# Cross-attention on one core: value products on stacked high and low parts, row sums on GpSimd, low probabilities on VectorE

## What is computed

```python
lat = layer_norm(latents, ln_lat_g, ln_lat_b)          # 4 x 128 x 512
ctx = layer_norm(context, ln_ctx_g, ln_ctx_b)          # 4 x 2048 x 512
q = (lat @ Wq).reshape(b, n, 16, 64).transpose(0, 2, 1, 3)
k, v = jnp.split(ctx @ Wkv, 2, axis=-1)                # 16 heads of 64 each
k = apply_rope(k, cos, sin)
attn = jnp.einsum('bhnd,bhsd->bhns', q, k) * 64 ** -0.5
attn = jax.nn.softmax(jnp.clip(attn, -11.0, 11.0), axis=-1)
out = jnp.einsum('bhns,bhsd->bhnd', attn, v)
```

## Time and profile before

| | us |
|---|---|
| median of three runs | 1448.81 |
| lowest, highest | 1445.45, 1450.21 |
| the profiled execution | 1454.4 |
| its span, first to last instruction | 1452.7 |
| the attention loop in it | about 83 to 1150 |

### The profile page before, as it was taken

How to read it: one execution, slowest core, us unless ns; L and a number is a source line. 1 busy time by engine, 2 the same in 40 slices (tenths; PEclk the granted TensorE clock), 3 DMA queues, 4 the chain that set the end, 5 groups by cost and what they waited for, 6 DMA issues and landing times. The chain is left out here.

```text
span 1452.7 us, 25242 instructions
## 1 busy us (share of the span) xinstructions
PE 1394.5 (96%) x8758; PEld 1139.3 (78%) x8758; DVE 850.0 (59%) x1420; ACT 797.3 (55%) x1237; POOL 833.6 (57%) x723
## 2 busy tenths in 40 slices
PE   5899999999999999999999999999998889999998
PEld 3578888888788888878888888888887566766664
DVE  6456565666466566655565666656554356657564
ACT  3356566665566665656666656656555312346652
POOL 3267677776667776766777777777765324110002
PEclk9999999999999999999999999999999989899999
DMA  7567766766666676656677666776767380369994
GB/s 241 178 118 130 123 118 110 132 116 135 114 120 123 111 130 110 139 100 129 113 131 122 123 130 118 130 123 107 138 107 163 116 326 0 131 219 365 357 370 150
DMA packets 115219, 218.44 MB, mean 150 GB/s; under 512 B 13312, under 2 KB 49152, under 8 KB 108928
## 3 DMA queue, kind: packets, MB, share of 16 engines
q1 hardware_dynamic: 111920, 209.00, 63.8%
q0 software_dynamic: 1280, 4.20, 0.9%
q10 hardware_dynamic: 1872, 3.41, 0.6%
HBM read 132.67 MB, written 16.78 MB: 103 GB/s over the span
## 5 line engine op out<-in xcount | busy, mean ns | idle before, releaser
L605 POOL TENSOR_TENSOR p_parts<-probs,p_parts 128x512 fp32r<-128x512 f32 x256 | 340.3, 1349 | 252.2 <-ACT p_parts L660 252.2
L660 ACT ACTIVATE p_parts<-probs 128x512 fp32r<-128x512 f32 x256 | 147.7, 625 | 245.5 <-PE banks L914 237.9
L768 DVE TENSOR_TENSOR probs<-banks,probs 128x1024 f32<-128x1024 f32 x128 | 156.7, 1224 | 164.1 <-ACT probs L668 164.1
L709 ACT ACTIVATE probs<-probs 128x1024 f32<-128x1024 f32 x128 | 135.9, 1062 | 142.6 <-POOL probs L612 142.5
L866 PE MATMUL banks<-wv_hi,x_hi 128*128 128x512 f32 x512 | 208.5, 407 | 4.9 <-PEq L170 4.9
L867 PE MATMUL banks<-wv_lo,x_hi 128*128 128x512 f32 x512 | 202.8, 396 | 0.0
L881 PE MATMUL banks<-x_hi,wk_hi 128*128 128x512 f32 x512 | 201.8, 394 | 0.0
L868 PE MATMUL banks<-wv_hi,x_lo 128*128 128x512 f32 x512 | 201.8, 394 | 0.0
L883 PE MATMUL banks<-x_hi,wk_lo 128*128 128x512 f32 x512 | 199.6, 390 | 0.0
L882 PE MATMUL banks<-x_lo,wk_hi 128*128 128x512 f32 x512 | 199.3, 389 | 0.0
L910 PE MATMUL banks<-p_parts,v_hi 128*65 128x128 f32 x1024 | 192.0, 224 | 0.6 <-POOL p_parts L605 0.6
(11 more groups left out here) (291 smaller groups left out, 2694.5 us busy)
## 6 DMA issues: line engine op xcount, KB each, us to landing
queries<-q_scratch SPq DMA_DIRECT2D x256, 128.0 KB, 6.0
keys<-wo_room SPq DMA_DIRECT2D x128, 256.0 KB, 5.6
keys<-turned_odd SPq DMA_DIRECT2D x128, 256.0 KB, 5.6
row_room<-in_ctx SPq DMA_DIRECT2D x64, 256.0 KB, 6.2
wo_room<-in_down SPq DMA_DIRECT2D x10, 1024.0 KB, 7.1
...
```

Source lines behind the costliest of these rows:

```text
L605: nc.gpsimd.tensor_tensor(p_parts[:, 1, j, :], probs[:, pair % 2, j, :], p_parts[:, 0, j, :].bitcast(F32), ALU.subtract).then_inc(p_lo_rea ...
L768: nc.vector.tensor_tensor(mine, ps_s[:, :, :, 0, :].rearrange("p j i n -> p (j i) n"), mine, ALU.add).then_inc(s_taken, 1)
```

## The change

Four things. **Values:** `v_parts` holds the high and the low part of a head's values side by side, 128 columns, with no column of ones; one product takes them both by the high and low parts of the probabilities, which now lie side by side in `p_parts` (256 columns). Its output has 128 partitions, 64 of high values and 64 of low values, by 256 columns. The quarter of low by low is computed and left unused. 8 products in place of 24. **Row sums:** GpSimd adds the probabilities of a pair over the four row tiles and the chunks into `totals` by three additions (`add_halves`, `add_totals`), and `turn_sums` turns those too. **Low probabilities:** one subtraction of 1024 elements on VectorE, between the normalisation and `take_scores`; the high part is one copy on ScalarE. **Sums:** `add_values` adds the left half of the bank into all 128 partitions of `acc` and then the right half (low probabilities) of the upper 64 (high values); `finish` adds the two halves of partitions after the turn. To make room, the queries have two slots instead of four, and each pair's load is issued in a step of its own.

```diff
-QUERY_SLOTS = 4
+QUERY_SLOTS = 2
...
-        v_lo = sb("v_lo", [P, ROW_TILES, HEADS, DHEAD], F32R)
         queries = sb("queries", [P, QUERY_SLOTS, 2, 2, QUERIES], F32R)
         probs = sb("probs", [P, 2, 2, CHUNK])
-        p_parts = sb("p_parts", [P, 2, 2, CHUNK], F32R)
-        acc = sb("acc", [DHEAD + 1, HEADS, QUERIES])
...
+        acc = sb("acc", [2 * DHEAD, HEADS, QUERIES])
+
+        totals = sb("totals", [P, HEADS, QUERIES])
+        halves = sb("halves", [P, 2, ROW_TILES // 2, QUERIES])
         recip = sb("recip", [P, 2])
+        total = sb("row_total", [P, 2])
...
-        sums = ps_o[0:DHEAD + 1, 0:2 * QUERIES].rearrange("p (j n) -> p j n", n=QUERIES)
+
+        sums = ps_o.rearrange("p (j w n) -> p j w n", j=2, n=QUERIES)
         rows["ps_tr"] = ps_o.rearrange("p (t n) -> p t n", n=P)
-        turned_sums = ps_s[:, 0, 0:2, 0, 0:DHEAD + 1]
+        turned_sums, turned_totals = ps_s[:, 0, 0:2, 0, :], ps_s[:, 0, 0:2, 1, :]
...
+                    wait(sp, k_ready, BATCH * BSTEPS - STEPS)
...
+                if exists(b, t - 2):
+
+                    if exists(b, t - SCORE_LAG):
+                        wait_alone(sp, s_ready, b * BSTEPS + (t - SCORE_LAG + 1))
+                    load_queries(b, t - 2)
+                if isinstance(b, int) and b == BATCH - 1:
+                    early_loads(t)
...
-                    if exists(b, t - 3):
-
-                        wait_alone(sp, s_ready, b * BSTEPS + (t - SCORE_LAG))
...
-                    for pair in (t - 3, t - 2):
-                        if exists(b, pair) and exists(b, t - 2):
-                            load_queries(b, pair)
-                    if exists(b, t - 2) and not exists(b, t):
-
-                        load_queries(b, t - 1)
...
-            def low_probs(b, pair):
+            def add_halves(b, pair):
+
                 if exists(b, pair):
-                    for j in range(2):
-                        wait(pool, p_hi_ready, b * (2 * BSTEPS) + (2 * pair + j + 1))
-                        nc.gpsimd.tensor_tensor(p_parts[:, 1, j, :], probs[:, pair % 2, j, :], p_parts[:, 0, j, :].bitcast(F32),
-                                                ALU.subtract).then_inc(p_lo_ready, 1)
+                    mine = probs[:, pair % 2].rearrange("p j (i n) -> p j i n", n=QUERIES)
+                    wait(pool, probs_ready, b * BSTEPS + (pair + 1))
+                    wait(pool, totals_ready, 2 * (b * BSTEPS + pair))
+                    nc.gpsimd.tensor_tensor(halves[:], mine[:, :, 0:2, :], mine[:, :, 2:4, :], ALU.add).then_inc(halves_ready, 1)
+
+            def add_totals(b, pair):
+                if exists(b, pair):
+                    n = b * BSTEPS + pair
+                    m = pair % STEPS
+                    mine = totals[:, 2 * m:2 * m + 2, :]
+                    wait(pool, halves_ready, n + 1)
+                    if pair // STEPS % CHUNKS == 0:
+                        for j in range(2):
+                            nc.gpsimd.tensor_tensor(mine[:, j, :], halves[:, j, 0, :], halves[:, j, 1, :], ALU.add).then_inc(totals_ready, 1)
+                    else:
+                        nc.gpsimd.tensor_tensor(halves[:, :, 0, :], halves[:, :, 0, :], halves[:, :, 1, :], ALU.add).then_inc(totals_ready, 1)
+                        wait(pool, totals_ready, 2 * n + 1)
+                        nc.gpsimd.tensor_tensor(mine, mine, halves[:, :, 0, :], ALU.add).then_inc(totals_ready, 1)
...
-                low_probs(b, t - VALUE_LAG)
+                add_halves(b, t - VALUE_LAG)
+                add_totals(b, t - VALUE_LAG)
                 clip(b, t - SCORE_LAG)
...
-                    for j in range(2):
-                        nc.scalar.activation(p_parts[:, 0, j, :], probs[:, pair % 2, j, :], ACT.Copy).then_inc(p_hi_ready, 1)
+                    nc.scalar.activation(p_parts[:, :, :, 0, :].rearrange("p j i n -> p (j i) n"),
+                                         probs[:, pair % 2].rearrange("p j (i n) -> p (j i) n", n=P), ACT.Copy).then_inc(p_hi_ready, 1)
...
-                    wait(act, p_lo_ready, b * (2 * BSTEPS) + (2 * pair - 2))
+                    wait(act, p_lo_ready, b * BSTEPS + (pair - 1))
+                    wait(act, halves_ready, b * BSTEPS + (pair - 1))
...
+                    below = acc[0:DHEAD, 2 * m:2 * m + 2, :]
                     wait(dve, o_ready, n + 1)
                     if pair // STEPS % CHUNKS == 0:
-                        nc.vector.tensor_copy(mine, sums).then_inc(o_added, 1)
+                        nc.vector.tensor_copy(mine, sums[:, :, 0, :]).then_inc(o_added, 1)
                     else:
-                        wait(dve, o_added, n - (STEPS - 1))
-                        nc.vector.tensor_tensor(mine, sums, mine, ALU.add).then_inc(o_added, 1)
+                        wait(dve, o_added, 2 * (n - (STEPS - 1)))
+                        nc.vector.tensor_tensor(mine, sums[:, :, 0, :], mine, ALU.add).then_inc(o_added, 1)
+                    wait(dve, o_added, 2 * n + 1)
+                    nc.vector.tensor_tensor(below, sums[0:DHEAD, :, 1, :], below, ALU.add).then_inc(o_added, 1)
+
+            def low_probs(b, pair):
+                if exists(b, pair):
+                    wait(dve, p_hi_ready, b * BSTEPS + (pair + 1))
+                    high, low = (p_parts[:, :, :, w, :].rearrange("p j i n -> p (j i) n") for w in range(2))
+                    nc.vector.tensor_tensor(low, probs[:, pair % 2].rearrange("p j (i n) -> p (j i) n", n=P), high.bitcast(F32),
+                                            ALU.subtract).then_inc(p_lo_ready, 1)
...
-                    nc.vector.reciprocal(recip[:], turned_sums[:, :, DHEAD]).then_inc(recip_ready, 1)
+                    there = keep["attn_last"][:, m * P:(m + 1) * P] if last_batch(b, pair) else attn[:, m % 2, :]
+                    there = there.rearrange("p (j e) -> p j e", j=2)
+                    nc.vector.tensor_reduce(total[:], turned_totals, AX_X, ALU.add)
+
+                    nc.vector.tensor_reduce(there, turned_sums.rearrange("p j (w e) -> p j e w", w=2), AX_X, ALU.add).then_inc(whole_ready, 1)
+                    wait(dve, whole_ready, done + 1)
+                    nc.vector.reciprocal(recip[:], total[:]).then_inc(recip_ready, 1)
                     wait(dve, recip_ready, done + 1)
-                    there = keep["attn_last"][:, m * P:(m + 1) * P] if last_batch(b, pair) else attn[:, m % 2, :]
                     for j in range(2):
-                        out = nc.vector.tensor_scalar(there[:, j * DHEAD:(j + 1) * DHEAD], turned_sums[:, j, 0:DHEAD],
-                                                      recip[:, j:j + 1], None, ALU.mult)
+                        out = nc.vector.tensor_scalar(there[:, j, :], there[:, j, :], recip[:, j:j + 1], None, ALU.mult)
...
+                low_probs(b, t - VALUE_LAG)
                 take_scores(b, t - SCORE_LAG)
...
             def turn_sums(b, pair):
                 if ends_batch(b, pair):
-                    wait(pe, o_added, b * BSTEPS + (pair + 1))
+                    wait(pe, o_added, 2 * (b * BSTEPS + (pair + 1)))
 
                     if exists(b, pair + 2):
                         wait(pe, s_taken, b * BSTEPS + (pair + 3))
+                    wait(pe, totals_ready, 2 * (b * BSTEPS + (pair + 1)))
                     for j in range(2):
-                        tr = nc.tensor.transpose(turned_sums[:, j, :], acc[:, 2 * (pair % STEPS) + j, :],
-                                                 keep["ident"][0:DHEAD + 1, 0:DHEAD + 1])
+                        nc.tensor.transpose(turned_totals[:, j, :], totals[:, 2 * (pair % STEPS) + j, :], keep["ident"][:])
+                    for j in range(2):
+                        tr = nc.tensor.transpose(turned_sums[:, j, :], acc[:, 2 * (pair % STEPS) + j, :], keep["ident"][:])
                     tr.then_inc(o_turned, 1)
 
             def weigh(b, pair):
                 if exists(b, pair):
                     m = pair % STEPS
-                    wait(pe, o_added, b * BSTEPS + pair)
+                    wait(pe, o_added, 2 * (b * BSTEPS + pair))
                     tile = row_tile_of(b, pair + VALUE_LAG)
                     if tile is not None:
 
                         wait(pe, rows["full_ready"], b * ROWS_OF_BATCH + tile + 1)
                     wait(pe, v_stored, b * BSTEPS + (pair - m + 4 * (m // 4 + 1)))
+                    wait(pe, p_lo_ready, b * BSTEPS + (pair + 1))
                     for j in range(2):
-                        wait(pe, p_lo_ready, b * (2 * BSTEPS) + (2 * pair + j + 1))
                         for i in range(ROW_TILES):
-                            cols = slice(i * P, (i + 1) * P)
-                            nc.tensor.matmul(sums[:, j, :], v_hi[:, i, 2 * m + j, :], p_parts[:, 0, j, cols],
-                                             start=(i == 0), stop=False)
-                            nc.tensor.matmul(sums[0:DHEAD, j, :], v_lo[:, i, 2 * m + j, :], p_parts[:, 0, j, cols],
```

(5 more changed lines are left out.)

37 lines of the change are left out of this document (19 added, 18 removed).

## The result

| | before | after |
|---|---|---|
| median of four runs, us | 1449.51 | 1493.03 |
| lowest, highest | 1445.45, 1453.92 | 1491.41, 1495.08 |
| span of the profiled execution | 1452.7 | 1493.3 |

The change makes the kernel slower: ratio 1.030, 95% interval 1.0266 to 1.0335. The forecast was 1503, its range 1455 to 1540.

The account below looks back on a forecast made before the run. TensorE bounds the kernel; the change makes it wait on VectorE and GpSimd's shared path. Ordinary pairs +38 us, batch-ending pairs +14, last 13 steps +2: +54 on the median 1448.8 gives 1503 us, range 1455 to 1540.

Parts of the forecast that it names:

- The bound moves from TensorE to a chain over the shared path: Attention loop: GpSimd's sum of halves delays VectorE's normalisation, so TensorE waits 1.75 us in each pair of steps.
- the walk: Operation-by-operation timing of an even and odd step across the engines: pair 17.15 us against 16.32, +0.83.
- TensorE's saving: Value products of a step: 8 of 256 columns take 1.00 us in place of 1.46, saving 0.46.
- Who gets the path between rotation sum and low probabilities: Even step: GpSimd's third operation runs before VectorE's low probabilities, 2.46 to 3.68; score sum ends at 4.82.
- The ending pairs: Steps that end a batch: turning the sums waits for the score sum; pair 17.9 us, +1.15, 14 us over 12.
- Falls into its hole: Batch-ending steps: VectorE's longer finish, two reductions of 256 elements, fits its idle time before the next rotation.
- the even step's wait is swallowed by the wait of 1.75: Batch-ending pairs: the turn's wait of 0.6 or more adds nothing beside TensorE's wait ahead of the row tile's transposes.
- The overlap at the handover: VectorE and GpSimd exclude each other, but the second starts some 0.13 us ahead of the other's end.
- The queries' two slots: Query loads, issued at step t and used at t + 2, some 15 us later: costed at nothing.
- The normalisation gets the port first: Rival, 12%: VectorE's normalisation goes ahead of GpSimd's sum of halves; pair 16.2 us, -0.1; total 1461.
- TensorE stays the bound: Rival, 15%: in the attention loop the normalisation is done by 9.6; pairs last 15.40 us, total 1404.
- Heavier: Rival, 11%: GpSimd's strided reads and two semaphore waits cost 0 to 0.2 us each; +0.4 a pair, about 1540.

Follow-up runs that it names:

- c1: Changed kernel with the sum of halves waiting for the normalisation, the finish's multiplications on ScalarE and low probabilities behind the low values: 1415.3 us, ratio 0.976.

## Why the prediction held, and which steps of it were off

- **The bound moves from TensorE to a chain over the shared path: shown.** The releaser of the wait ahead of the transposes, the normalisation at 1.49 us and the start of the sum of halves 0.02 before the rstd's end are as forecast, and the kernel that lets the normalisation go first takes the stretch away. The wait itself is smaller: 1.14 us by the records, below the 1.2 to 1.9 that I had named, where the walk had 1.75; and in the ending pairs it is hardly there.
- **TensorE's saving: right, a little too small.** Eight value products take 0.94 us, forecast 1.00. The score products, which were the measure, now take 0.96 themselves. The formula of the Trainium skill (TensorE: Matmul & The Clock Gate, "Back-to-back issue gap"), columns over 2.4 GHz plus 2.5 ns, would have had 0.87, an estimate; this case's trace, at a granted clock of 0.99, lies between.
- **Who gets the path between rotation sum and low probabilities: wrong.** The forecast let GpSimd's addition in, with low probabilities from 2.46 and the score sum until 4.82. In this pair VectorE went from one to the other without giving the path away: low probabilities from 1.86, score sum until 4.20, and GpSimd's L618 waited out both. From there to the rstd the step gave a little back (the clip, beside the second rotation sum, took 1.48), so that the rstd ended at 9.43 instead of 9.81. The turn began 0.06 behind the normalisation, where the walk had 0.24, at 11.02 instead of 11.6. The pair lasted 16.58, not 17.15: this term was 0.83 us a pair and measured 0.26 to 0.33. For the 46 ordinary pairs that made 38 us; the 32 steady ones and the 12 behind a batch's end measured 14.5.
- **The ending pairs: too small.** "Falls into its hole" was the step that failed: VectorE had no hole. So was "the even step's wait is swallowed by the wait of 1.75": the even step's turn waits 1.89, and the transposes behind it wait 0.24 at most. The stretch between 317 and 336 us has 17.85 us of work on VectorE in 19. I had priced the two reductions, but took the two multiplications as unchanged, though they now read SBUF and not PSUM; behind GpSimd's halves they take 2.05 us. So the rotation began at 0.56 instead of -0.71 and the score sum ended at 5.50, not at 4.2 to 4.8. The term was 1.15 us a pair, 14 us; it measured 2.02, 24 us. (Two times of that walk, 13.6 and 12.9, don't agree with 14.2 and about 13.5 of the walk for the steady pair; their difference, 0.7, is the same.)
- **The overlap at the handover: held.** The normalisation ended 0.28 after the sum of halves, and L618 0.60 after the low probabilities, less than the 0.74 it needs alone. With the exclusive lock held to the letter (SBUF — State Buffer, "SBUF: two separate sides", of the Trainium skill) no operation would show less than its own length behind the other; the trace shows 0.27 and 0.14 us less. That one of the two blocks the other the trace bears out. That the one that starts first gets the path it does not, if starts are taken from the records (see the last section).
- **The rest.** The queries' two slots cost nothing that shows. Ahead of the loop and behind it 3.7 us were added that I had not counted. Two errors of opposite sign (-23 and +10 us) met, so the total (+54 forecast, +40.6 between the spans, +43.5 between the medians) is better than its parts; that is luck.
- **The rivals.** "The normalisation gets the port first" was given 1461; the kernel that forces it took 1471.6. The difference is in the main the ending pairs again, +1.84 instead of +1.2, and the 3.7 us outside the loop. "TensorE stays the bound" (1404) is what c1 nearly reaches, 1415.3, by order and by the finish on ScalarE. "Heavier" had up to 0.2 us for each of GpSimd's two waits for itself; they take 0.08 (464.50 to 464.58, 467.23 to 467.31).
